# A sequence mixer whose output projection runs one pipeline step later, with its scratch zeroed on the way and its step loops written out

## What is computed

```python
mod = silu(c) @ wmod                              # six rows per sequence: sa, ca, ga, sb, cb, gb
h  = layernorm(x) * (1 + ca) + sa
# the mixer (a state-space layer, 16 heads of 64, chunks of 128 tokens):
xn = h * rsqrt(mean(h*h)) * norm_w
z, xBC, dt = split(xn @ in_proj_w.T)              # 1024 + 1280 + 16 columns
xBC = silu(causal_conv4(xBC)); dt = softplus(dt + dt_bias)
y  = Y_diag(chunk) + Y_off(state of the chunks before) + D * xs
y  = y * silu(z);  y = y * rsqrt(mean(y*y)) * gnorm_w
x1 = x + ga * (h + y @ out_proj_w.T)
# the feed-forward part (64 experts, 8 for each token, and a shared one):
h2 = layernorm(x1) * (1 + cb) + sb
topk_w, topk_idx = route(h2)                      # grouped top 8
out = x1 + gb * (sum over 8 experts + shared)(h2)
```

## Time and profile before

| | before |
|---|---|
| time, median of 3 (us) | 6647.73 |
| profiled execution: its own time | 6649.34 |
| its span in the trace | 6647.6 |
| busy: TensorE (PE) | 5827.6 (88%) |
| busy: VectorE (DVE) | 3962.2 (60%) |
| busy: ScalarE (ACT) | 2731.6 (41%) |
| busy: GpSimd (POOL) | 3636.9 (55%) |
| mean granted TensorE clock | 0.938 |

### The profile page before, as it was taken

One profiled execution on the slowest core, in us unless ns is written; L12 is line 12 of the kernel. 1 busy time (PEld: TensorE's weight loads), 2 busy tenths in 40 slices (PEclk: granted clock), 3 DMA queues, 4 the chain that ended last, 5 costly groups with the idle time before them and its releaser, 6 DMA issues. The chain is left out here.

```text
span 6647.6 us, 115164 instructions
## 1 busy us (share of the span) xinstructions
PE 5827.6 (88%) x28797; PEld 4395.7 (66%) x28798; DVE 3962.2 (60%) x10033; ACT 2731.6 (41%) x5780; POOL 3636.9 (55%) x2980
## 2 busy tenths in 40 slices
PE   2878888888878888888877999999999999999999
PEld 1555555555555555555545888888888888888777
DVE  1878887887877878778873444444344444444345
ACT  1544444454544444445432333333333333333322
POOL 0455555555555555555564555555555555555567
PEclk8889898998889989899988999999999999999999
DMA  9333233333333332333236787787777777887677
GB/s 345 107 116 107 101 102 118 117 106 101 102 114 116 110 101 100 103 115 116 101 106 160 193 228 190 177 229 173 191 189 174 192 154 169 234 211 192 110 256 256
DMA packets 338087, 1027.13 MB, mean 155 GB/s; under 512 B 55060, under 2 KB 59412, under 8 KB 337124
## 3 DMA queue, kind: packets, MB, share of 16 engines
q1 hardware_dynamic: 175512, 669.44, 28.9%
q0 software_dynamic: 145568, 321.56, 24.5%
q10 hardware_dynamic: 16816, 34.37, 1.4%
HBM read 580.45 MB, written 444.74 MB: 154 GB/s over the span
## 5 line engine op out<-in xcount | busy, mean ns | idle before, releaser
L1332 POOL DMA_INDIRECT acc_dram<-y_e,ids x576 | 907.2, 1575 | 1116.0 <-ACT y_e L1405 688.8
L1213 PE MATMUL bank<-w_hi,x_hi 128*128 (+1 forms) x2560 | 1058.0, 413 | 0.0
L1213 PE MATMUL bank<-w_hi,x_lo 128*128 (+1 forms) x2560 | 1002.9, 392 | 0.0
L1213 PE MATMUL bank<-w_lo,x_hi 128*128 (+1 forms) x2560 | 1001.8, 391 | 0.0
L946 DVE SCALAR_TENSOR_TENSOR acc<-raw,conv_w,acc 128x128 f32<-128x128 f32 x1920 | 804.6, 492 | 48.8 <-ACT acc L673 46.7
L778 PE MATMUL bank<-xn_t,w_in 128*128 128x128 f32 x5120 | 645.9, 292 | 214.0 <-ACT xn_t L652 214.0
L778 PEld LDWEIGHTS bank<-xn_t,w_in 128*128 128x128 f32 x5120 | 633.7, 207 | 229.4 <-ACT xn_t L652 229.4
L610 POOL DMA_INDIRECT list_dram<-tok_id,pos x512 | 615.2, 1202 | 155.5 <-issue 154.5
L1423 DVE TENSOR_TENSOR h_lo<-bank,h_hi 128x256 fp32r<-128x256 f32 x576 | 243.8, 423 | 763.9 <-ACT h_hi L1394 763.6
L1405 ACT ACTIVATE y_e<-bank,xg_e 128x512 f32<-128x512 f32 x576 | 396.0, 688 | 693.2 <-PE bank L1213 693.2
L1324 POOL DMA_INDIRECT xg_e<-h_dram,ids x576 | 571.5, 992 | 195.2 <-issue 174.6
(11 more groups left out here) (248 smaller groups left out, 10901.1 us busy)
## 6 DMA issues: line engine op xcount, KB each, us to landing
hi_dram<-w_hi_m SPq DMA_DIRECT2D x130, 768.0 KB, 3.3
lo_dram<-w_raw SPq DMA_DIRECT2D x130, 768.0 KB, 6.2
w_hi<-hi_dram SPq DMA_DIRECT2D x130, 768.0 KB, 7.3
w_lo<-lo_dram SPq DMA_DIRECT2D x130, 768.0 KB, 10.3
w_raw<-in_w_experts_dram SPq DMA_DIRECT2D x128, 768.0 KB
acc_dram<-zeros ACTq DMA_DIRECT2D x2, 16640.0 KB, 102.1
acc_c<-acc_dram SPq DMA_DIRECT2D x128, 256.0 KB, 3.4
h_dram<-h SPq DMA_DIRECT2D x64, 288.0 KB, 3.8
```

Of the source, the lines that this page charges most:

```text
L1213: last = nc.tensor.matmul(acc, a, b, start=(i == 0), stop=(i == len(terms) - 1))
L1332: pool.indirect_dma_start(acc_dram[r % NACC], bass.IndirectOffsetOnAxis(ap=ids[:, r:r + 1], axis=0), y[:, r % YSLOTS, :], None, compute_op ...
```

## The change

A sixth stage `o` = s-1 is put between `c` and `t`, which become s and s-2; `q` becomes s-3 and the steps run to 66. Of chunk c's work, the transposes of `y`, the projection with `w_out` (now into `half(3)`), the copy `y_t` and the whole of `x1` with its statistics move to stage `o`, one step later and to other places of the lists. On VectorE the three operations that finish `y`, which stood right after `state`, now stand behind the routing of chunk t, and `dt` stands ahead of the scaling of the picked weights. `xg` gets a third slot. On ScalarE, `y_t`, `h2_t`, `trt` and the square of `h` change places. All steps are written out, so that no engine has a loop in the mixer. The zeros are no longer written at the start but in the steps, 2 x 256 KB in each, from SyncE's queue. The tables, the experts and the final sum are the same instructions as before. Cut to its core:

```diff
                     act.dma_start(h2_dram[TOKENS:TOKENS + P, :], zeros[:]).then_inc(s_zero, 16)
-                    for dram in acc_dram:
-                        act.dma_start(dram.rearrange("(p n) d -> p n d", p=P),
-                                      zeros[:, 0:DM].unsqueeze(1).to_broadcast([P, TOKENS // P + 1, DM])).then_inc(s_zero, 16)
...
-                step(*(v if 0 <= v < NCH else None for v in (s + 2, s + 1, s, s - 1, s - 2)), s % 2,
+                step(*(v if 0 <= v < NCH else None for v in (s + 2, s + 1, s, s - 1, s - 2, s - 3)), s % 2,
...
-            for s in range(-2, 2):
-                one(s)
-            cuts = [2, *between, NCH - 4]
...
-                with eng.Fori(a, b - 1, 2) as s:
...
-            for s in range(NCH - 4, NCH + 2):
+            for s in range(-2, NCH + 3):
+                if s in between:
+                    between[s]()
                 one(s)
...
                     if ws is not None:
+                        for dram in acc_dram:
+                            sp.dma_start(rows_of(dram, ws), zeros[:, 0:DM]).then_inc(s_zero, 16)
                         split_load(sp, ws, 1)
...
-                        at_least(pool, S["x1_done"], e - 1)
-                        pool.wait_ge(S["h_done"], e + 1)
-                        nc.gpsimd.tensor_tensor(xg[:, p, :], h[:], modrow(G_A, e), ALU.mult).then_inc(S["xg_half"], 1)
+                        at_least(pool, S["x1_done"], e - XGS + 1)
+                        wait_apart(pool, S["h_done"], e + 1, passed)
+                        nc.gpsimd.tensor_tensor(xg_of(e), h[:], modrow(G_A, e), ALU.mult).then_inc(S["xg_half"], 1)
...
-                        at_least(pe, S["x1_done"], c)
+                        at_least(pe, S["yoff_sb"], c)
```

More of the change, by code:

```diff
@@ L712, in step @@
                         nc.scalar.activation(xbc[:, 1 - p, :, :], acc[:], ACT.Tanh).then_inc(S["conv_th"], 1)
+                    if e is not None:
+                        act.wait_ge(S["h_done"], e + 1)
+                        at_least(act, S["rr_done"], e)
+                        nc.scalar.activation(junk[:, 0:DM], h[:], ACT.Square, accum_out=ssq[:]).then_inc(S["ssq_done"], 1)
+                    if t is not None:
+                        act.wait_ge(S["h2T_ps"], t + 1)
+                        at_least(act, S["rt_ps"], t)
+                        nc.scalar.copy(h2_t[:].rearrange("p k t -> p (k t)"), half(5)).then_inc(S["h2T_sb"], 1)
+                    if t is not None:
+                        act.wait_ge(S["rt_ps"], t + 1)
+                        at_least(act, S["sc_done"], t)
+                        nc.scalar.activation(trt[:], half(4)[:, RT:RT + EXPERTS], ACT.Tanh, scale=0.5).then_inc(S["rt_th"], 1)
                     if e is not None:
@@ L798, in step @@
                         last.then_inc(S["yoff_ps"], 1)
-                        pe.wait_ge(S["btok_sb"], c + 1)
-                        pe.wait_ge(S["small_sb"], c + 1)
+                    if o is not None:
+                        pe.wait_ge(S["yT_sb"], o + 1)
+                        if c is not None:
+                            pe.wait_ge(S["l_exp"], 2 * c + 2)
+                        for i in range(KI):
+                            last = nc.tensor.matmul(half(3), y_t[:, i, :], w_out[:, i, :], start=(i == 0), stop=(i == KI - 1))
+                        last.then_inc(S["out_ps"], 1)
+                    if t is not None:
+                        pe.wait_ge(S["h2_done"], t + 1)
+                        if o is not None:
+                            pe.wait_ge(S["yT_sb"], o + 1)
+                        for k in range(KD):
+                            last = nc.tensor.transpose(half(5)[:, k * P:(k + 1) * P], h2[:, p, k * P:(k + 1) * P], ident[:])
+                        last.then_inc(S["h2T_ps"], 1)
                     if t is not None:
@@ L832, in step @@
                             last.then_inc(S["z_ps"], 1)
-                    if c is not None:
-                        pe.wait_ge(S["y_done"], c + 1)
-                        pe.wait_ge(S["state_done"], c + 1)
-                        for i in range(KI):
-                            last = nc.tensor.transpose(bank[2][:, i * P:(i + 1) * P], y[:, i * P:(i + 1) * P], ident[:])
-                        last.then_inc(S["yT_ps"], 1)
                     if t is not None:
@@ L845, in step @@
                         nc.tensor.matmul(half(2)[:, EXPERTS:2 * EXPERTS], ones_bf[:], picked[:], start=True, stop=True).then_inc(S["rank_ps"], 1)
-                    if c is not None:
-                        pe.wait_ge(S["yT_sb"], c + 1)
-                        pe.wait_ge(S["yoff_sb"], c + 1)
-                        for i in range(KI):
-                            last = nc.tensor.matmul(half(7), y_t[:, i, :], w_out[:, i, :], start=(i == 0), stop=(i == KI - 1))
-                        last.then_inc(S["out_ps"], 1)
                 steps(pe, step)
```

193 lines of the change are left out of this document (97 added, 96 removed).

## The result

| | median (range) of the runs | ratio to the kernel before, 95% interval |
|---|---|---|
| before | 6647.9 us (6642.66 to 6648.12) | 1 |
| changed | 6901.41 us (6842.77 to 6963.61, four runs) | 1.030 (1.0275 to 1.0324) |

The kernel became 3.0% slower. Two of its four runs, near 6960 us, were disturbed and are left out of the ratio; the others took 6842.77 and 6848.86 us, and the profiled execution is the first (span 6840.8 us).

What follows compares the result with a forecast made beforehand. A closed chain through POOL's fixed order (`hn2`, DVE to `y`, list DMAs, `xg`, `nm2`) was taken as the bound, 56.0 us a step. Mixer +257, start -54, tail +22 give +225 on 6649.3: 6875 us, range 6780 to 7020.

Steps and rivals of the forecast that it cites:

- the side that had 0.82: Whole kernel: the chance given to the change making it slower, against 0.01 for same and 0.17 for faster.
- start: Set-up before the mixer: zeros no longer written there, so `xin` issues sooner; -54 us, bounds 35 to 75.
- tail: End of the mixer: eight more list DMAs in series and one more uncovered pass; +22 us, between 0 and 40.
- `hn2` to `y`: Mixer step, DVE's way from `hn2` to the end of `y`: 37.4 us where it was 26.4.
- the eight list DMAs: POOL's part of the mixer step: 12.1 us for eight, as before the change.
- `xg` to the end of `nm2`: End of POOL's chain in a step: 3.7 us, as beside an idle DVE, instead of 6.1.
- 60 steps, less 3: Mixer from step 3 to 63: 60 steps of 56.0, less 3 for the last without `xg`; +257 us.
- `r2e` idle for about 20: Sign on POOL in the mixer: `r2e` idle for about 20 us instead of 10.02.
- DVE waiting some 10 ahead of `lm`: Sign on DVE in the mixer: some 10 us of waiting ahead of `lm`, and never for `x1`.
- A lower granted clock in the mixer: Sign in the mixer: the granted clock would be lower after the change; no size given.
- rival 4: Mixer: straight code isn't free, PE or POOL stalls at new instructions, say 3 us a step; 7055 and up, chance 0.07.
- The step that failed: Mixer without POOL's bound: ScalarE's order gives 50 us a step, 6515 us, chance 0.12; later `x1` then worth DVE's idle time.

Runs made afterwards that it cites:

- e4: The kernel before with all mixer steps written out, no loops, nothing else changed: 6406.09 us, ratio 0.9663.
- e7: The kernel before with steps written out and accumulators zeroed in the steps, so the change without its stage: 6349.32 us, ratio 0.9575.
- e1: The changed kernel with `r2` moved behind the list DMAs and `xg` in POOL's step: 6803.0 us, ratio 1.0261.
- e8: The changed kernel with the eight list DMAs moved to the head of POOL's step, right behind `nm2`: 6785.77 us, ratio 1.0231.
- e9: e8 with ScalarE's sixteen `lm` of the next chunk also moved ahead of the square of `y`: 6787.77 us, ratio 1.0236.
- e2: The changed kernel with DVE's three `y` operations moved right behind `state`, ahead of the routing: 6803.36 us, ratio 1.0262.
- e3: The changed kernel with the moves of e1 and e2 together: 6968.78 us, ratio 1.0514.
- e13: e1 with the output projection moved behind the rank matmuls and DVE's `x1` block behind `pos`: 6902.87 us, ratio 1.0408.
- e10: e8 with `rs1` and `nm1` moved right behind the list DMAs: 6908.01 us, ratio 1.0422.
- e12: The changed kernel with only DVE's `key` and `nbase` moved directly behind `y`: 6977.98 us, ratio 1.0523.
- e6: The changed kernel with loops of two steps again, from step 6 to 59: 7025.41 us, ratio 1.0605.

## Why the prediction was right, and where it wasn't

**The result and its terms.** Forecast 6875 us, +225 on the profiled execution; measured +193 in the span and 3.0% in the ratio, inside the range and on the side that had 0.82. The mechanism is the one forecast: in all 29 steps between 1200 and 2800 us `hn2` is released by POOL's `nm2`, after a wait of 4.2 us or more, and the chain adds up. The error of the total, 32 us too much, is that of the mixer's steps alone; the small ones of start, first steps, tail and what lies behind cancel, which is luck.

| term | forecast | measured |
|---|---|---|
| `hn2` to `y` | 37.4 | 37.8 (mean) |
| `y` to the first list DMA | 2.4 | 2.6 |
| the eight list DMAs | 12.1 | 11.1 |
| `xg` to the end of `nm2` | 3.7 | 3.75 |
| step | 56.0 | 55.4 |
| 60 steps, less 3 | +257 | +225 |
| start | -54 | -56.5 (step 0 starts at 127.61, was 184.08) |
| steps 0 to 3 | 0 | +3.4 |
| tail | +22 | +27 |

The rest of the difference, -6, lies behind the mixer. The one term off in size is the list DMAs, 11.1 for 12.1 us; with 0.4 more on `hn2` to `y` it makes the 0.6 us a step, and the 32 us over 60 steps. The 0.4 are the wait for the states, 1.0 in the mean where I took 0.5. In the step shown three of the eight DMAs are longer than 0.96 (1.09, 1.35, 1.77).

By the Trainium skill, "SBUF — State Buffer", section "SBUF: two separate sides", GpSimd can't write descriptors while DVE holds the shared port pair; I had worked out from it that DMAs beside an idle DVE take the short time, which gave 54.4 a step. The trace agrees in that: all 87 that lie beside an idle DVE between 1200 and 2800 us took 0.95 to 0.97. The step is still 55.4, since more than one of the eight meets DVE at work: those beside `x1s` took 1.58 in the mean, those beside the split `w_raw` 1.16.

**What was to be seen.** `r2e` idle for about 20: 14.5, and 5.9 ahead of `rre` before it, which I had not split off. `hn2` waiting some 5 for `nm2`: 5.0 in the mean (271.5 / 54). DVE waiting some 10 ahead of `lm`: 8.7; in the steps never for `x1`. First `xin` near 87: 84.97. A lower granted clock in the mixer: no, 0.90 as before; but the kernel before has its loops in that, and beside e4, which ran at 0.93 from 1200 to 2800 us, it is lower. No "issue" waits on DVE at a loop's head: right.

**Straight code** (rival 4) cost nothing that can be seen: e4 and e7 gained what the loops cost. The loops' price in the kernel before was 3.9 us a step, where I had 4.4 to 5.3: the steps 60 to 63 that I took for a measure, at 46.6, are a little shorter than written-out steps in the middle, 47.8.

**The step that failed** is one that the result did not depend on. I wrote that with POOL out of the way ScalarE's order would give 50 us a step, and that `x1` a step later would then be worth DVE's idle time. `y` to `hn2` over ScalarE is indeed 12.5 us (e1), and the step is 55.2. So POOL's chain does close the step of the changed kernel, but opening it (e1, e8, e9) or shortening it (e2) gained less than a microsecond a step, 0.4 to 0.7%. I had taken `hn2` to `y` as a constant of 37.4, computed with the states ready 0.5 us late, the softplus undisturbed and the conv at its old length. In e1 it is 42.7: DVE's wait for the states 2.3 us, the softplus 3.0 us longer, since `xg` ahead of `y` meets it. TensorE, which waits 2.8 us for `y_t` in the changed kernel, comes later to `h_t` there, waits less for it (2.6 us in the mean, 3.2 in e1) and is oftener at full clock behind it. In e8, where `xg` stays behind `y`, it is 42.0: the conv ends 3.3 us later, by 3.0 us more in its taps.

**What the stage costs and where** is shown in sum (7.6%, changed against e7) and by piece: conv end to `y` went from 5.9 to 17.4 us, and `y` to `hn2` from 21.4 to 17.6. Of the 11.5, `xbc`, `x1`, the routing and softplus ahead of `y` are the larger part (2034.69 and 2039.0 to 2044.93 in the rows), the wait for the states the smaller, 1.0 us in the mean. Moving `y` back ahead of the routing doesn't return them: `dta` and `lm` then stand behind `y` (e3), or the list DMAs meet the routing (e2).

**What the other orders have in common** is in part shown. In most of them POOL's work and DVE's come to stand beside each other where they had not. POOL's products lengthen DVE's softplus (e1 and e13, about 3 us) or its taps (e8 and e10, 3 to 4 us), or DVE's operations lengthen the list DMAs (e2 1.7 us, e12 0.9). These sizes are read from the traces; no run has removed such a meeting alone. The other cause is that router and states hang on `h_t` behind the conv's tanh. In every kernel with the stage that was traced, the router starts 2.4 us behind the start of the tanh, and the states are ready 5.8 us (full clock) to 8.5 us (half) behind it. What DVE waits for them bounds what that costs it directly: 1.0 us a step in the changed kernel, 2.3 in e1, 5.7 in e13. No run has moved `h_t` alone, so what moving it would return is argued, not shown. Why TensorE ran more at the lower clock in e12, and by what way POOL held `y` in e3, stay open too.

## What to carry to other kernels

- A chain that adds up to the step tells what the step is, not what removing it is worth. Before counting on the next longest chain, its pieces must be added up again with the instructions where they will then stand: an operation moved out of one chain runs beside another and lengthens it (`xg` beside the softplus, `x2s` beside the taps), and an engine that gets done sooner waits longer and comes back at the lower clock.
- A wait that a trace shows need not be what holds the result up. In e8 the wait for `nm1` looked like the cause of the late conv, and e10, which removed it, left the conv as late; the mean duration of one tap showed the cause.
- Idle time ahead of one instruction is spare only for that one: what is shifted into it runs beside other work (e6), and a copy such as `h_t` late in a list holds up a whole engine (e13).
- Of three edits tried together, two were good: without the stage the kernel takes 0.9575 of the time before, and no single time of the whole change could show it.
